# Moving a normalised tile into a PSUM bank and letting two transposed operands share another

## The reference

```
rk = normalised heads of layernorm(x);  wk = rk of the token before
v, gate, beta = projections of layernorm(x)
for every token t:
    pred = wk_t S;  err = (v_t - pred) * beta_t
    S = S + wk_t (outer) err;  o_t = (rk_t S) * gate_t
x1 = x + layernorm(o @ Wo.T)
xn = (layernorm(x1) - mu) * rsqrt(var + 1e-3) * ln_gamma + ln_beta
gamma = max |xn| over the whole tensor        # one scale for the quantisation
y = clip(xn * 128 / gamma) @ ternary(weight) * scale
out = x1 + layernorm(y)
```

## Time and profile before

| | |
|---|---|
| median of 3 runs | 2558.0 us (2552.95 to 2560.36) |
| time of the profiled execution | 2552.82 us |
| its span from first to last instruction | 2551.1 us |
| mean granted TensorE clock | 0.947 |
| attention steps with a `rhs` | 128, the first at 146.8 us, the last at 2052.7 us |
| DVE busy | 2239.5 us, 88% |
| PE busy | 2161.4 us, 85% |

### The profile page before, as it was taken

How to read it: one execution, slowest core, us unless ns; L and a number is a source line. 1 busy time by engine, 2 the same in 40 slices (tenths; PEclk the granted TensorE clock), 3 DMA queues, 4 the chain that set the end, 5 groups by cost and what they waited for, 6 DMA issues and landing times. The chain is left out here.

```text
span 2551.1 us, 146840 instructions
## 1 busy us (share of the span) xinstructions
PE 2161.4 (85%) x61989; PEld 1350.0 (53%) x61989; DVE 2239.5 (88%) x6603; ACT 1699.0 (67%) x3372; POOL 1731.3 (68%) x2841
## 2 busy tenths in 40 slices
PE   1679999999999999999999989999998747777776
PEld 1356555556555565555655555556655524434442
DVE  4599999999999999999999999999999837777875
ACT  2667777777777777777777777777774335555554
POOL 1556777767777776777777767776775335777777
PEclk7789999999999999999999999999999868888888
DMA  2112222222222222222222222222222124565554
GB/s 79 51 46 63 71 79 76 75 71 72 78 72 78 72 75 72 75 78 71 75 76 78 72 71 78 77 74 71 73 66 62 53 95 146 152 162 153 153 139 99
DMA packets 132137, 215.50 MB, mean 84 GB/s; under 512 B 31352, under 2 KB 31360, under 8 KB 131488
## 3 DMA queue, kind: packets, MB, share of 16 engines
q1 hardware_dynamic: 131488, 206.20, 28.4%
HBM read 104.40 MB, written 67.11 MB: 67 GB/s over the span
## 5 line engine op out<-in xcount | busy, mean ns | idle before, releaser
L740 DVE TENSOR_TENSOR ps_elim<-ps_elim,sys 128x30 f32<-128x30 f32 (+14 forms) x1920 | 543.4, 326 | 0.8
L748 DVE TENSOR_TENSOR sys<-sys,ps_elim 128x30 f32<-128x30 f32 (+14 forms) x1920 | 534.4, 316 | 1.0
L893 PE MATMUL ps_v<-wv,xt 128*128 128x512 f16 x1536 | 433.5, 391 | 34.7 <-DMA kbd<-kt 20.5
L893 PE MATMUL ps_y<-wo,ot 128*128 128x512 f16 x1536 | 404.3, 387 | 12.4 <-DVE x L811 10.1
L1293 PE MATMUL ps_f<-wq,f_xq 128*128 128x512 f16 x1024 | 281.6, 426 | 102.1 <-ACT f_yn L1169 97.5
L920 PEld LDWEIGHTS ps_chain<-rhs,t_t 32*32 32x32 f32 x16384 | 263.1, 144 | 127.0 <-issue 121.7
L543 POOL TENSOR_TENSOR o_g<-pred,gate 128x512 f32<-128x512 f32 x128 | 134.3, 1049 | 286.1 <-DVE pred L827 286.1
L920 PE MATMUL ps_chain<-rhs,t_t 32*32 32x32 f32 x16384 | 294.5, 218 | 20.2 <-issue 12.8
L620 ACT ACTIVATE z<-x,z_sc 128x512 f32<-128x512 f32 x128 | 104.1, 814 | 265.4 <-POOL z_sc L519 265.4
L528 POOL TENSOR_TENSOR m_t<-gram,b_mask 128x512 f32<-128x512 f32 x128 | 164.3, 1283 | 147.7 <-ACT gram L627 141.7
L914 PEld LDWEIGHTS ps_chain<-state,key_t 32*32 32x32 f32 x16384 | 174.5, 105 | 158.2 <-issue 156.4
(11 more groups left out here) (155 smaller groups left out, 5157.7 us busy)
## 6 DMA issues: line engine op xcount, KB each, us to landing
x_in<-in_L_attn_x SPq DMA_DIRECT2D x128, 256.0 KB
kbd<-kt SPq DMA_DIRECT2D x512, 64.0 KB
x_res<-in_L_attn_x SPq DMA_DIRECT2D x128, 256.0 KB
x_scratch<-x SPq DMA_DIRECT2D x128, 256.0 KB, 6.4
f_x<-x_scratch SPq DMA_DIRECT2D x32, 1024.0 KB, 7.6
out<-f_res SPq DMA_DIRECT2D x128, 256.0 KB, 3.9
gate<-gates SPq DMA_DIRECT2D x128, 7.9 KB
gate<-gates SPq DMA_DIRECT2D x128, 0.2 KB
```

The lines of the kernel that those rows point to most:

```text
L740: dve.tensor_tensor(tmp, factors(r, c, first, end)[:, c - first:C - 1 - first, c - first:c - first + 1].to_broadcast(shape), sys[:, r, c:c ...
L748: dve.tensor_tensor(dst, dst, tmp, ALU.add).then_inc(elim_done[r], 1)
L893: last = pe.matmul(out, lhs[:, a, kb, :], weights[:, w, kb, :], start=(i == 0), stop=(i == 3 * KB - 1))
```

## The change

It takes three steps that belong together. The bank that was `ps_ot` becomes `ps_zn`, and ACT writes z there in place of SBUF; DVE reads it from there. There is one buffer instead of two, so ACT waits for the extremes of the tile before, and z moves to the end of the ACT step. The turned output goes into the bank of the Gram matrix, and its transposes on PE move from ahead of the turning of x to behind the state update, its copy on ACT from ahead of `xt` to behind `state`.

```diff
-        z = sb("z", [P, 2, D])
-        ps_ot, ps_v = bank("ps_ot"), bank("ps_v")
+        ps_zn, ps_v = bank("ps_zn"), bank("ps_v")
+        ps_ot = ps_gram
 ACT:
-   (after rn0, before gram)
-                    wait(act, s["max_done"], n)
-                    wait(act, s["min_done"], n)
-                    nc.scalar.activation(z[:, l % 2, :], x1[:, l % 4, :], ACT.Identity, ...)
-   (after err, before xt)
-                    wait(act, s["ot_psum"], n + 1)
-                    wait(act, s["y_psum"], n - 1)
-                    nc.scalar.activation(ot[...], ps_ot[:, :].bitcast(F16), ACT.Copy)
+   (after state, before g_exp): the same wait and copy of ot
+   (after g_exp, at the end of the step)
+                    wait(act, s["z_scale"], n + 1)
+                    wait(act, s["max_done"], n + 1)
+                    wait(act, s["min_done"], n + 1)
+                    wait(act, s["x1_done"], n + 1)
+                    nc.scalar.activation(ps_zn[:, :], x1[:, l % 4, :], ACT.Identity, ...)
 DVE:
-                    dve.tensor_tensor(k["z_ends"][:, 0, :], z[:, l % 2, :], k["z_ends"][:, 0, :], ALU.max)
+                    dve.tensor_tensor(k["z_ends"][:, 0, :], ps_zn[:, :], k["z_ends"][:, 0, :], ALU.max)
-                    dve.tensor_tensor(k["z_ends"][:, 1, :], z[:, l % 2, :], k["z_ends"][:, 1, :], ALU.min)
+                    dve.tensor_tensor(k["z_ends"][:, 1, :], ps_zn[:, :], k["z_ends"][:, 1, :], ALU.min)
 PE:
+   gram_ready:      wait(pe, s["ot_done"], upto(j - 1 + LAG_OUT + 1))
+   before turning x: wait(pe, s["ot_done"], upto(j - 1 + LAG_OUT + 1))
-   (before turning x): the eight transposes into ps_ot
+   (after the second half of the update)
+                    wait(pe, s["ot_done"], n)
+                    wait(pe, s["xt_done"], upto(j + LAG_TURN + 1))
+                    wait(pe, s["gram_done"], upto(j + LAG_GRAM + 1))
+                    wait(pe, s["olo_done"], n + 1)
+                    the same eight transposes into ps_ot
```

More of the change, by code:

```diff
@@ L611, in step @@
                                          bias=k["rn_bias"][:, 0:1]).then_inc(s["rn0_done"], 1)
-                n, l, live = on(base, j, LAG_Z)
-                if live:
-                    wait(act, s["z_scale"], n + 1)
-                    wait(act, s["max_done"], n)
-                    wait(act, s["min_done"], n)
[L618 to L621, removed]
                 n, l, live = on(base, j, LAG_GRAM)
@@ L640, in step @@
                     nc.scalar.activation(err[:, :], ps_chain[:, :], ACT.Copy).then_inc(s["err_done"], 1)
-                n, l, live = on(base, j, LAG_OUT)
-                if live:
-                    wait(act, s["ot_psum"], n + 1)
-                    wait(act, s["y_psum"], n - 1)
-                    nc.scalar.activation(ot[:, l % 2, :, :, :].rearrange("p a k t -> p (a k t)"), ps_ot[:, :].bitcast(F16),
-                                         ACT.Copy).then_inc(s["ot_done"], 1)
                 n, l, live = on(base, j, LAG_TURN)
@@ L668, in step @@
                     nc.scalar.activation(state[:, (l + 1) % 2, :], ps_s[:, :], ACT.Copy).then_inc(s["state_done"], 1)
+                n, l, live = on(base, j, LAG_OUT)
+                if live:
+                    wait(act, s["ot_psum"], n + 1)
+                    wait(act, s["y_psum"], n - 1)
+                    nc.scalar.activation(ot[:, l % 2, :, :, :].rearrange("p a k t -> p (a k t)"), ps_ot[:, :].bitcast(F16),
+                                         ACT.Copy).then_inc(s["ot_done"], 1)
                 n, l, live = on(base, j, LAG_V)
@@ L674, in step @@
                                          scale=k["gate_unit"][:, 0:1]).then_inc(s["gexp_done"], 1)
+                n, l, live = on(base, j, LAG_Z)
+                if live:
+                    wait(act, s["z_scale"], n + 1)
+                    wait(act, s["max_done"], n + 1)
+                    wait(act, s["min_done"], n + 1)
+                    wait(act, s["x1_done"], n + 1)
+                    sc = z_sc[:, l % 2, :]
+                    nc.scalar.activation(ps_zn[:, :], x1[:, l % 4, :], ACT.Identity,
+                                         scale=sc[:, 0:1], bias=sc[:, 1:2]).then_inc(s["z_done"], 1)
             nc.scalar.preload_act_table_set("natural_log_exp_and_others")
@@ L818, in step @@
                     dve.wait_ge(s["max_done"], n + 1)
-                    dve.tensor_tensor(k["z_ends"][:, 0, :], z[:, l % 2, :], k["z_ends"][:, 0, :], ALU.max).then_inc(s["max_done"], 1)
+                    dve.tensor_tensor(k["z_ends"][:, 0, :], ps_zn[:, :], k["z_ends"][:, 0, :], ALU.max).then_inc(s["max_done"], 1)
                     dve.wait_ge(s["min_done"], n + 1)
-                    dve.tensor_tensor(k["z_ends"][:, 1, :], z[:, l % 2, :], k["z_ends"][:, 1, :], ALU.min).then_inc(s["min_done"], 1)
+                    dve.tensor_tensor(k["z_ends"][:, 1, :], ps_zn[:, :], k["z_ends"][:, 1, :], ALU.min).then_inc(s["min_done"], 1)
                 n, l, live = on(base, j, 0)
@@ L878, in gram_ready @@
                 if live:
+                    wait(pe, s["ot_done"], upto(j - 1 + LAG_OUT + 1))
                     wait(pe, s["xt_done"], upto(times(base, BODY, j + LAG_TURN)))
@@ L952, in step @@
                     last.then_inc(s["err_psum"], 1)
[L954 to L962, removed]
                 n, l, live = on(base, j, LAG_TURN)
@@ L1007, in step @@
                     last.then_inc(s["s_psum"], 1)
+                n, l, live = on(base, j, LAG_OUT)
+                if live:
+                    wait(pe, s["ot_done"], n)
+                    wait(pe, s["xt_done"], upto(j + LAG_TURN + 1))
+                    wait(pe, s["gram_done"], upto(j + LAG_GRAM + 1))
+                    wait(pe, s["olo_done"], n + 1)
+                    for a in range(2):
+                        for kb in range(KB):
+                            last = pe.transpose(ps_ot[:, :].bitcast(F16)[:, D * a + P * kb:D * a + P * kb + P],
+                                                o_part[:, l % 2, a, P * kb:P * kb + P], k["ident_half"][:, :])
+                    last.then_inc(s["ot_psum"], 1)
                 if v_live:
```

## The result

The changed kernel takes 2649.42 us (median of 4 runs, 2644.82 to 2659.64), the kernel before 2559.18 (4 runs, 2552.95 to 2572.29). The ratio is 1.035, 95% interval 1.030 to 1.040: 90 us slower, where I forecast 30 faster. The profiled execution took 2659.64 us, its span is 2657.9. The mean granted TensorE clock fell from 0.947 to 0.927.

What follows compares the result with a forecast made beforehand. PE bounds the kernel, DVE close behind. 32.8 us of waits go and 3 come back: 29.9 us a pair of steps instead of 30.4, 30 us over 59 pairs, giving 2528 against the median 2558.0; range 2503 to 2563.

Steps and rivals of the forecast that it cites:

- the paragraph on gram: ACT copies gram right after rn0, so PE's 26.8 us wait goes; POOL's m_t and o_part start sooner, nobody waiting for them.
- the lock: Between DVE and POOL: a DVE operation with two SBUF inputs waits until POOL is through; one with a PSUM input doesn't.
- the 5.97 us from rhs to the end of x1: DVE's time from the start of rhs to x1's end in the even step, a term of the odd-to-even loop.
- Turned output behind the update: PE's eight transposes, 0.62 us, moved behind the update: PE's total the same, update's end 0.62 us sooner after the prediction.
- two "issue" groups: PE's two largest stalls that no semaphore explains, 37.2 and 32.9 us; their growth would show the prediction wrong.
- 0.41 us a pair: Saving on DVE from L819 falling from 882 to 679 ns because it reads z from PSUM.
- Slower: Rival: ACT's late L556 delays POOL's ln_mean, the key, and DVE's g_den and rhs; 41 us slower, 2600; chance 0.14.
- The late L556: ACT's next step starts behind ot and z: ln_sum read about 3.15 us after the update's end, 1.43 before.
- T gets ahead of P: PE's update end (T) passing DVE's pred end (P): T comes 1.1 us earlier in all, outweighing a 0.7 us delay.
- No change: Rival: PE's wait for gram becomes one for x1, no stall hidden, 30.5 us a pair, 2551 to 2565; chance 0.14.
- the prediction's own sign of being wrong: PE's waits for x1 passing 30 us; under 10 us were expected.
- the 14.7 us loop: From odd update's end to even one's, through ACT, POOL, DVE's x1 and PE: 14.7 us, 0.74 over PE's 13.99.

Runs made afterwards that it cites:

- Experiment 5: Kernel before with ACT's gram block swapped ahead of z, nothing else: 2612.38 us, ratio 1.019.
- Experiment 1: Changed kernel plus one wait on POOL, so that m_t can't start ahead of DVE's key norm L800: 2537.47 us, ratio 0.991 to the kernel before.
- experiment 8: Changed kernel with m_t's wait for the key norm, and z on ACT moved behind the next step's ln_sum: 2540.62 us, ratio 0.991 to the kernel before.
- experiments 3: Kernel before with z alone moved, unchanged in SBUF, to the end of ACT's step: 2610.95 us, ratio 1.019.
- 4: Kernel before with the turned output alone moved behind the update on PE and behind state on ACT, in its own bank: 2569.29 us, ratio 1.003.
- 10: Kernel before with both z and the turned output moved late, z in SBUF and the turned output in its own bank: 2641.70 us, ratio 1.037.
- experiment 2: Changed kernel with z back in SBUF in two buffers, at the same late place: 2653.40 us, ratio 1.034 to the kernel before.
- 7: Changed kernel with m_t's wait for the key norm and z back in SBUF: 2550.12 us, ratio 0.994 to the kernel before.
- experiment 11: Kernel before with gram and z swapped on ACT and m_t waiting for DVE's key norm: 2513.58 us, ratio 0.986.

## Why the prediction was wrong

**The step that failed** is in the paragraph on gram: "POOL's m_t and o_part also start sooner, and nobody waits for them". I asked who waits for their results. The question was whom they hold while they run. I had described the lock earlier in the same text, and had read L779, L819 and g_den by it (g_den, a tensor_scalar with one SBUF input, does not even fit the rule as I wrote it), but did not lay POOL's two instructions, moved 1.16 us forward, over DVE's list. The distance was there to read, from POOL's two rows of the kernel before above, and these two, the last key norm of the odd step and L789 of the even one:

```profile
1010.24 0.17 DVE L800 SCALAR_TENSOR_TENSOR rn<-rn_t,rn 128x16 f32<-128x16 f32 x1
...
1026.07 0.17 DVE L789 SCALAR_TENSOR_TENSOR rn_t<-rn_t,ss 128x16 f32<-128x16 f32 x1
```

In the even step x1 starts at 1026.51, with the key norms just ahead of it. The m_t at 1027.05, moved forward by 1.16, begins at 1025.89, ahead of L789, and holds it. In the odd step, from 1012.23 to 1011.07, it still comes after the key norms, which are over at 1010.4. That is why one step in two is hit. The changed kernel bears it out: m_t starts 0.24 us ahead of L789 in the even steps and 0.94 behind it in the odd ones (medians; 0.97 and 2.18 behind it in the kernel before), and of PE's 50 waits for x1 from 200 to 1900 us all are in even steps. The term of the sum that was too small for it is the 5.97 us from rhs to the end of x1: it took 7.63. Experiment 5 has this with gram moved alone: 1.9%. Experiment 1 shows that without it the change gains 0.9%.

**The price was doubled by a second step**: "Turned output behind the update: ... moved and not removed, so PE's total is the same". By itself that is nearly right (0.3%). But with the 0.62 us of transposes taken from ahead of the output projection, PE comes to it sooner and meets the late x1 with less cover: the wait for x1 is 58.5 us from 200 to 1900 with z late alone, and 94.0 with both. What adds to it is TensorE's clock. With z late alone a wait for x1 lasts 1.2 us on average (61.8 us in 51 waits from 200 to 2080) and the clock over the stage is 0.99. With both it lasts 1.9 us (101.9 in 55), longer by about the 0.62 us of the transposes, the clock is 0.97, and PE's own work takes 0.28 us a step more than in the kernel before. That the longer wait brings the clock down is read from the stretches above; no run varied the wait's length by itself. What part the late ln_sum has in this doubling is open too: ln_mean waits 23.5 us with z late alone and 91.9 with both, and the ln_sum was brought forward only in a kernel with m_t's wait (experiment 8). The two parts cost 1.9% and 0.3% alone and 3.7% together (experiments 3, 4, 10).

**What was right.** L819 at 680 ns; PE's waits for gram gone and for kbd nearly (0.9 us left), 32.8 us before; no growth of the two "issue" groups (28.9 and 24.4 us); the reading of z from PSUM as dear as from SBUF (678 and 675 ns), against the 62 cycles more in the table of the Trainium skill (page "VectorE: DVE Perf Modes", the TRN2 errata); the write of z at 0.80 us; the waits added on PE and ACT covered; the ln_sum at T + 3.2. But the gain that I put down to PSUM, 0.41 us a pair, comes with z in SBUF as well in the new order, in which o_part is over by then: 680 ns in experiment 2, 690 in 7.

**The rivals.** "Slower" had the right sign by the wrong mechanism. The late L556 was there (ln_mean waits 91.9 us from 200 to 1900), yet experiments 1 and 8 have it, or half of it, at no cost, and experiment 5 has a loss of 1.9% without it. Its argument against, that T gets ahead of P, held only in the odd steps: T was 0.78 us ahead of P there and 0.52 behind it in the even ones (medians), where x1 is late. "No change" named the right wait, PE's for x1, and the prediction's own sign of being wrong, such waits past 30 us, came (99.9), but not its source: the rival took the 14.7 us loop at its bare length and put PE's stalls on top, while what made it longer were the held key norms inside it.

**The mechanism of the gain** that I forecast exists. The changed kernel with the lock avoided takes 2537 us; I had said 2528. Since the wait on POOL by itself gives 0.4%, about half of that is the change's own, by my estimate. It is the earlier gram that brings it, and needs no bank to be moved: experiment 11 has it with gram and z swapped and m_t's wait.

## What to carry to other kernels

When a queue is freed and an engine starts sooner, lay the instructions that move over the list of every engine that they can hold, not only over the list of those that wait for them: between POOL and DVE that is each DVE instruction with two SBUF inputs, be it on 16 columns, and in this kernel the tensor_scalar ones with a single one too. Of such a held instruction ask what stands behind it in its queue; here moving one instruction ahead of the held ones took away the loss (0.994) nearly as well as avoiding the lock (0.991). A wait that looks like a loss (POOL standing 1.16 us for gram) may be what keeps two engines apart; take it out only together with an explicit wait in its place.

## What the runs showed of the hardware

A DVE operation on 128 x 16 elements, 0.17 us by itself, took 1.07 and 1.09 us beside POOL instructions with SBUF inputs, and ended 0.03 us after each of them. This held for scalar_tensor_tensor as well as tensor_tensor, and for tensor_scalar with one SBUF input: L796 took up to 1.27 us beside m_t, and g_den (L842) up to 1.05 beside the key, against a shortest of 0.15. x1 and pred, with one input from PSUM and one from SBUF, and the reduction L785 never took more than 0.02 us over their shortest in the changed kernel. The Trainium skill's page "SBUF — State Buffer" ("Who interferes with whom") calls the lock exclusive. It has a DVE instruction with two SBUF inputs contend with a GpSimd instruction that reads SBUF, and the rows agree. The prediction gave the other half of it without its condition: the page exempts an instruction with one SBUF input only outside the "2-port perf modes", and counts tensor_scalar among those that can enter them; L796 and g_den agree with that. The granted clock of TensorE fell to 0.50 in a standstill of 1.93 us, stayed there for about three microseconds, and was 0.98 again from 1009.4. Behind another of 2.29 us, at 1038.21, the same three matmuls took 0.82 us at a granted clock of 1.00, so not each such wait brought it down.
